# Three-stage seams of a fused attention and routed-leaf kernel: weights, rows and gathers issued in the stage before, output groups and an inverse moved between VectorE and POOL

## The chip, the cores and the metric

The kernel runs on one core of one Trainium2 chip. The metric is the device time of one execution in microseconds. Before the change the median of three runs is 4000.38 us (3998.59 to 4003.65). Engines: TensorE (PE, with its weight loads as PEld), VectorE (DVE), ScalarE (ACT), GpSimd (POOL), SyncE (SP), which only issues transfers here.

## The reference, cut to what matters

The input x is [8, 1024, 256] in float32. The output is x plus a differential attention and a fast-feedforward attention of the normalised x.

```python
xn = _layernorm(x)
# differential attention, 16 heads of 16, two maps per head
A1 = einsum('bhqd,bhkd->bhqk', Q1, K1) * scaling
A2 = einsum('bhqd,bhkd->bhqk', Q2, K2) * scaling
attn = softmax(A1) - lamb * softmax(A2)
out = einsum('bhqk,bhkd->bhqd', attn, V)          # then @ Wo, layernorm, gamma, beta
# feedforward: three trees (q, k, v), each token takes one of 16 leaves
cur = 2 * cur + 1 + (score >= 0)                  # four levels
hidden = relu(xf @ w1[leaf] + b1[leaf])           # 256 -> 64
y = hidden @ w2[leaf] + b2[leaf]                  # 64 -> 256
# then softmax(q k^T / 16) v per batch, over 1024 tokens
return x + attention(xn) + ffn_attention(xn)
```

## The kernel before

The program is four blocks that run one after the other, each with a barrier at its end: `route_stage` (layer norm, projections, routing of every token), `attention_stage`, `leaf_stage` and `mix_stage` (the softmax over the leaf outputs). Each block takes its own SBUF memory, and gives it back at its end; what passes between them goes through scratch tensors in HBM.

**Attention** handles 64 sets, eight of each of the eight batches; a set is two heads with two maps each, so four parts. A set has 16 steps (two halves of 512 queries, eight key tiles each). In a step TensorE writes four score tiles, ScalarE takes their exponentials (L1488), and TensorE multiplies by the values (L1358). For a later set TensorE writes row scores in advance (L1304) into one of three auxiliary banks, four a step, and VectorE reduces each to a row maximum (L1631) before the bank is free again. The same three banks carry the "extras", in an order written out by hand (`extras`, `GROUP_PLACES`, L1141): at step 5 and step 11 the finished values of a half are turned (`"o"`, `turn_o`), at step 12 the shift for the next set, and in sets 0 and 1 of a batch the turning and projection of the two output groups of the batch before. ScalarE reads a turned half with `read_o` (L1454). VectorE then inverts the row sums at step 7 or 13 (`invert`, L1641), and POOL multiplies by sign and inverse and adds the two maps (`join_maps`, L1528 to L1536); the result goes to `oset`, which the output groups are made of.

An output group is 512 tokens. VectorE takes its statistics in set 1 of the next batch, at step 1 (group 0) and step 14 (group 1), with `stats` (L1758 to L1763). POOL does the rest in `finish`: five small operations for the inverse deviation, beginning with a power (L1770 to L1778), and five over 4 x 256 columns (L1780 to L1793). SP stores the group. After the last batch both groups are done in the same way in an epilogue, and the block ends when the stores have landed. In the first half of a batch POOL also scatters the normalised rows to their sorted places (`scatter`, L1539).

**Leaf** runs over 240 tiles of 128 sorted tokens, 80 for each tree. A tile's leaf has a record of 641 words in SBUF; POOL copies the record of each tile out of all 16 (`choose`, L819) into a ring of eight (`WBUF`), and may be eight tiles ahead of VectorE. TensorE turns a pair of tiles (L757), multiplies by the first weights (L768) and the second (L779) in this order: turn of pair p, hidden of p - 1, output of p - 2. VectorE adds the bias (L835) into one of four store buffers (`YBUF`) of four tiles. SP issues loads of rows six groups of four tiles ahead (`XAHEAD`), the stores, and the weights of a tree, 5.25 MB, of which two sets fit:

```python
load(0)
nc.sync.dma_start(leafw[:, 0], w["leafw"][0]).then_inc(leafw_in[0], 16)
for g in range(1, XAHEAD):
    load(g)
nc.sync.dma_start(leafw[:, 1], w["leafw"][1]).then_inc(leafw_in[1], 16)
```

**Mix** takes one batch after the other. POOL gathers the rows of q, k and v with one indirect transfer for each 128 tokens (L919), eight of them for one input of a batch. TensorE turns q and k (`turn_rows`, L942), ScalarE and VectorE split them in two parts (L1002, L133), and scores, exponentials, turned probabilities and values follow.

Of the kernel before, what the change touches and what calls it, by code (L numbers as in the profile page):

```python
# [75 lines left out]
ROUTE_WORDS, LEAF_WORDS, MIX_WORDS, ATTENTION_WORDS = 38900, 40000, 21200, 40000  # L76
# [606 lines left out]
def leaf_stage(nc, ctx, ps, w, scratch):  # L683
# [3 lines left out]
    leafw = ar.take(2, LEAVES, REC)  # L687
    ident = ar.take(P)
    tablei = ar.take(TILES_ALL).bitcast(I32)
    xg = ar.take(XBUF, GROUP_T, DIM)  # L690
# [8 lines left out]
    leafw_in = [sem(f"leafw{f}_in") for f in range(NFFF)]  # L699
    ident_in, table_in = sem("ident_in"), sem("table_in")  # L700
    xg_in, y_stored = [sem(f"xg{n}_in") for n in range(XBUF)], [sem(f"y{n}_stored") for n in range(YBUF)]
# [13 lines left out]
    with nc.Block() as block:  # L715

        @block.sync
        def _(sp):
            nc.sync.dma_start(tablei[0:1], scratch["table"]).then_inc(table_in, 16)
            nc.sync.dma_start(ident, w["ident"]).then_inc(ident_in, 16)  # L720

            def load(g):
                if g >= XBUF:

                    sp.wait_ge(xT_full, (g - XBUF + 1) * GROUP_T // 2)
                tokens = scratch["sorted_x"][GROUP_T * P * g:GROUP_T * P * (g + 1)]
                nc.sync.dma_start(xg[:, g % XBUF], tokens.rearrange("(t p) d -> p t d", p=P)).then_inc(xg_in[g % XBUF], 16)

            load(0)
            nc.sync.dma_start(leafw[:, 0], w["leafw"][0]).then_inc(leafw_in[0], 16)  # L730
            for g in range(1, XAHEAD):
                load(g)
            nc.sync.dma_start(leafw[:, 1], w["leafw"][1]).then_inc(leafw_in[1], 16)
            for g in range(GROUPS):
                if g + XAHEAD < GROUPS:
                    load(g + XAHEAD)
                if (g + 1) * GROUP_T == TILES_F:

                    sp.wait_ge(wsel_ready, TILES_F)
                    nc.sync.dma_start(leafw[:, 0], w["leafw"][2]).then_inc(leafw_in[2], 16)  # L740
# [7 lines left out]
        def _(pe):  # L748
            def turn_pair(p):
# [5 lines left out]
                for n in range(2):  # L755
                    for k in range(KC):
                        last = nc.tensor.transpose(bank(p % 2)[:, (KC * n + k) * P:(KC * n + k + 1) * P],  # L757
                                                   xg[:, g % XBUF, 2 * p % GROUP_T + n, k * P:(k + 1) * P], ident)
# [24 lines left out]
            pe.wait_ge(ident_in, 16)  # L783
# [29 lines left out]
        def _(pool):  # L813
            def choose(n):
# [4 lines left out]
                nc.gpsimd.tensor_copy(wsel[:, n % WBUF], leafw[:, n // TILES_F % 2, bass.ds(leaf, 1)].rearrange("p a n -> p (a n)")  # L819
                                      ).then_inc(wsel_ready, 1)  # L820

            pool.wait_ge(table_in, 16)
# [16 lines left out]
def mix_stage(nc, ctx, ps, w, scratch, out):  # L839
# [4 lines left out]
    rows = ar.take(2, 2, TT, DIM)  # L844
# [4 lines left out]
    ident = ar.take(P)  # L849
    posi = ar.take(TOK_TILES, NFFF).bitcast(I32)  # L850
# [1073 lines left out]
```

## Time and profile before

| | us |
|---|---|
| median of three runs | 4000.38 |
| the profiled execution | 4000.26 |
| its span | 3998.4 |
| PE busy | 3750.3 (94%) |
| DVE busy | 3155.2 (79%) |
| ACT busy | 2784.6 (70%) |
| POOL busy | 1111.7 (28%) |

The page cuts the span in 40 slices of 100 us. Route is the first four, attention ends early in slice 32, the leaf stage ends in slice 34 and mix takes the rest. A share of busy time over the whole is an average over these stages; an engine's digit in a slice says what it does in that stage. Times in the rows are microseconds from the start of the span; "[... <-X]" behind a row is the idle time of the engine before it and what ended it.

### The profile page before, as it was taken

What the parts mean: (1) busy time and instruction counts of PE and PEld (TensorE: products, weight loads), DVE (VectorE), ACT (ScalarE), POOL (GpSimd) and SP (SyncE); (2) the same over time, 40 slices, a digit from 0 to 9 for tenths busy, and PEclk for the clock granted to TensorE, in tenths of its full rate; (3) what the DMA queues carried; (4) which work ended last, traced back from release to release, by engine and by line L of the source; (5) the groups of instructions that cost most, each with busy time, mean ns of one, the idle gap of its engine ahead of it and who ended that gap; (6) DMA issues with size and microseconds to landing.
All of it is one profiled execution on the core that took longest, in us unless ns stands there. A gap on an engine that the chain in (4) does not pass through costs nothing. (4 is left out here: it accounts for less than half of the span.)

```text
span 3998.4 us, 63421 instructions
## 1 busy us (share of the span) xinstructions
PE 3750.3 (94%) x23714; PEld 1469.9 (37%) x23714; DVE 3155.2 (79%) x5549; ACT 2784.6 (70%) x3257; POOL 1111.7 (28%) x1552
## 2 busy tenths in 40 slices
PE   7998999999999999999999999999999859799999
PEld 5772222222222222222222222222222235488888
DVE  6548899999989999998999999899999323345444
ACT  4440788888888888887888888788878836522221
POOL 3321141132113113211311321131131267662330
PEclk9996999999999999999999999999999979899999
DMA  8883110111111011111101111110100079732220
GB/s 289 308 294 98 40 44 28 48 42 38 39 45 43 28 47 42 38 42 42 43 28 53 37 38 44 40 43 28 51 29 29 22 285 324 237 116 72 88 85 22
DMA packets 224694, 330.89 MB, mean 83 GB/s; under 512 B 29297, under 2 KB 165236, under 8 KB 219780
## 3 DMA queue, kind: packets, MB, share of 16 engines
q1 hardware_dynamic: 205668, 276.08, 21.4%
q0 software_dynamic: 18432, 50.36, 3.9%
q8 instruction: 190, 3.11, 0.3%
q14 instruction: 116, 0.95, 0.1%
q10 hardware_dynamic: 288, 0.39, 0.1%
HBM read 169.34 MB, written 156.34 MB: 81 GB/s over the span
## 5 line engine op out<-in xcount | busy, mean ns | idle before, releaser
L1631 DVE TENSOR_REDUCE arena<-psum 128x1 f32<-128x512 f32 x4096 | 2559.4, 682 | 171.9 <-PE psum L1304 155.2
L1488 ACT ACTIVATE arena<-psum,exp_scale 128x1024 f32<-128x1024 f32 x2048 | 2157.6, 1110 | 297.6 <-PE psum L1342 287.2
L1304 PE MATMUL psum<-arena 48*128 48x512 f16 x4096 | 1313.8, 394 | 112.9 <-DVE arena L1631 35.2
L1358 PE MATMUL psum<-arena 128*32 128x512 f32 x8200 | 1106.2, 612 | 1.2 <-ACT arena L1488 0.6
L1304 PEld LDWEIGHTS psum<-arena 48*128 48x128 f16 x4096 | 317.1, 93 | 1764.1 <-DVE arena L1631 1492.4
L1342 PE MATMUL psum<-arena 50*128 50x512 f16 x4096 | 901.5, 384 | 15.4 <-ACT arena L1488 8.4
L1528 POOL TENSOR_TENSOR arena<-arena 128x16 f32<-128x16 f32 x129 | 28.4, 220 | 2078.4 <-DVE arena L1641 2078.4
L1016 ACT ACTIVATE mix_arena<-psum,mix_arena 128x1024 f32<-128x1024 f32 x64 | 71.3, 1114 | 328.9 <-DVE mix_arena L1036 328.9
L1358 PEld LDWEIGHTS psum<-arena 128*32 128x32 f32 x8200 | 162.1, 108 | 257.3 <-issue 255.7
L1342 PEld LDWEIGHTS psum<-arena 50*128 50x128 f16 x4096 | 213.7, 95 | 93.2 <-ACT arena L1488 78.8
L919 POOL DMA_INDIRECT mix_arena<-scratch_sorted_y,mix_arena x192 | 181.7, 946 | 235.1 <-PE psum L971 168.7
L835 DVE TENSOR_TENSOR leaf_arena<-psum,leaf_arena 128x256 f32<-128x256 f32 x240 | 90.5, 420 | 183.5 <-PE psum L779 170.5
L971 PE MATMUL psum<-mix_arena 128*128 128x256 f32 x1024 | 232.5, 380 | 2.7 <-DVE qk_lo L133 2.7
L1539 POOL DMA_INDIRECT scratch_sorted_x<-arena x192 | 188.5, 982 | 54.9 <-issue 54.9
L971 PEld LDWEIGHTS psum<-mix_arena 128*128 128x128 f32 x1024 | 189.6, 190 | 28.8 <-DVE qk_lo L133 5.6
L819 POOL COPY leaf_arena<-leaf_arena 128x641 f32 x240 | 168.4, 722 | 81.2 <-issue 41.9
L1035 DVE TENSOR_REDUCE mix_arena<-psum 128x1 f32<-128x1024 f32 x64 | 78.4, 1225 | 129.7 <-PE psum L141 129.7
L460 ACT ACTIVATE route_arena<-psum,route_arena 128x512 f16<-128x512 f32 x128 | 88.4, 691 | 117.7 <-PE psum L141 117.7
L555 DVE SCALAR_TENSOR_TENSOR route_arena<-psum,route_arena 128x512 f16<-128x512 f32 x128 | 95.7, 749 | 56.4 <-ACT route_arena L460 55.6
L806 ACT ACTIVATE leaf_arena<-psum 128x512 f32<-128x512 f32 x120 | 71.7, 597 | 95.0 <-PE psum L757 95.0
L1051 DVE SCALAR_TENSOR_TENSOR mix_arena<-psum,mix_arena 128x256 f32<-128x256 f32 x64 | 31.0, 484 | 117.2 <-PE psum L971 117.2
L757 PE MATMUL psum<-leaf_arena 128*128 128x128 f32 x480 | 80.6, 292 | 35.9 <-DMA leaf_arena<-scratch_sorted_x 35.9
(167 smaller groups left out, 3311.9 us busy)
## 6 DMA issues: line engine op xcount, KB each, us to landing
arena<-scratch_split SPq DMA_DIRECT2D x762, 64.0 KB
scratch_split<-route_arena SPq DMA_DIRECT2D x64, 512.0 KB, 3.3
scratch_sorted_x<-route_arena SPq DMA_DIRECT2D x60, 512.0 KB, 4.5
leaf_arena<-scratch_sorted_x SPq DMA_DIRECT2D x60, 512.0 KB, 6.0
scratch_sorted_y<-leaf_arena SPq DMA_DIRECT2D x60, 512.0 KB, 4.0
leaf_arena<-in_leafw SPq DMA_DIRECT2D x3, 5128.0 KB, 18.8
arena<-in_x SPq DMA_DIRECT2D x18, 512.0 KB, 4.9
scratch_sum<-arena SPq DMA_DIRECT2D x18, 512.0 KB, 2.9
```

The source lines that it names most:

```text
L460: nc.scalar.activation(parts[:, p % SPLIT_RING, 0, cols], unit_bank("qk", b, u), ACT.Identity, scale=lift[:, t, a:a + 1]).then_inc(act_rea ...
L555: nc.vector.scalar_tensor_tensor(parts[:, n, 1, cols], unit_bank("qk", b, u), lift[:, t, a:a + 1], parts[:, n, 0, cols], ALU.mult, ALU.sub ...
L819: nc.gpsimd.tensor_copy(wsel[:, n % WBUF], leafw[:, n // TILES_F % 2, bass.ds(leaf, 1)].rearrange("p a n -> p (a n)")).then_inc(wsel_ready, 1)
L835: nc.vector.tensor_tensor(yg[:, g % YBUF, n % GROUP_T], bank(4 + 2 * (n // 2 % 2) + n % 2)[:, 0:DIM], wsel[:, n % WBUF, B2], ALU.add).then ...
L919: nc.gpsimd.indirect_dma_start(dst, None, scratch["sorted_y"], bass.IndirectOffsetOnAxis(ap=posi[:, at, f:f + 1], axis=0)).then_inc(gather ...
L971: last = nc.tensor.matmul(bank[:, 0:DIM], probT[:, t % 2, kt, :], v[:, b % 2, kt, :], start=kt == 0, stop=kt == TT - 1)
L1304: nc.tensor.matmul(aux_bank[bank], ring[at, slot, 0, m, qt * P:(qt + 1) * P], ring[at, slot, 1, m, c * CH:(c + 1) * CH], start=True, stop=True
L1342: last = nc.tensor.matmul(score[:, 2 * m + h, :], ring[at, s % RING, 1, m, kt * P:(kt + 1) * P], ring[at, s % RING, 0, m, c * CH:(c + 1) * ...
L1358: last = nc.tensor.matmul(value_bank[32 * j:32 * j + 32, :], vaug[:, batch % 2, kt, 2 * pair + j % 2, :], prob[:, step % 2, j, :], start=k ...
L1488: nc.scalar.activation(prob[:, step % 2, 2 * h:2 * h + 2, :], score[:, 2 * h:2 * h + 2, :], ACT.Exp, scale=exp_scale[:, s % 2, s // 2:s // ...
L1539: nc.gpsimd.indirect_dma_start(scratch["sorted_x"], bass.IndirectOffsetOnAxis(ap=token_places[:, t, f:f + 1], axis=0), token_rows[:, t], N ...
L1631: nc.vector.tensor_reduce(halfmax[:, odd, 2 * m + h, qt, c:c + 1], aux_bank[bank], AX.X, ALU.max).then_inc(bank_used[bank], 1)
```

## The change

The inverse of the row sums is computed on POOL at the head of `join_maps`, as a power of -1 and one Newton step, so four operations more on POOL, and VectorE's `invert` with its waits is gone. POOL waits for ScalarE's read of the turned half itself. The finish of an output group is cut in two: `inverse_std` (the five small operations) and `finish` (the five large ones), and after the last batch VectorE runs `finish` for both groups, behind their statistics.

Two sets of buffers outlive a stage. `LeafStart` holds the first tree's weights, the identity, the table of leaves and two groups of rows; SP issues the first three in set 2 of the last batch and the rows after the last set, once all scatters have landed. `MixStart` holds the places and the q and k rows of two batches; the places are loaded in the leaf stage behind the second weights, and the 16 gathers of batch 0's q and k are issued by POOL in the leaf stage, one after each record copy from tile 184 on.

```diff
+class LeafStart:
+    SLOTS = 2
+    def load_weights(self, eng, w, scratch):
+        eng.dma_start(self.tablei[0:1], scratch["table"]).then_inc(self.table_in, 16)
+        eng.dma_start(self.ident, w["ident"]).then_inc(self.ident_in, 16)
+        eng.dma_start(self.leafw, w["leafw"][0]).then_inc(self.leafw_in, 16)
+    def load_rows(self, eng, scratch, g):
+        tokens = scratch["sorted_x"][GROUP_T * P * g:GROUP_T * P * (g + 1)]
+        eng.dma_start(self.xg[:, g], tokens.rearrange("(t p) d -> p t d", p=P)).then_inc(self.xg_in[g], 16)
+class MixStart:
+    def gather(self, eng, scratch, dst, b, f, t):
+        at = TT * b + t
+        eng.indirect_dma_start(dst, None, scratch["sorted_y"][0:(f + 1) * TILES_F * P],
+                               bass.IndirectOffsetOnAxis(ap=self.posi[:, at, f:f + 1], axis=0)
+                               ).then_inc(self.gathered[f][b % 2], 16)
...
 leaf_stage, SP
-            load(0)
-            nc.sync.dma_start(leafw[:, 0], w["leafw"][0]).then_inc(leafw_in[0], 16)
-            for g in range(1, XAHEAD):
+            for g in range(start.SLOTS, XAHEAD):
                 load(g)
-            nc.sync.dma_start(leafw[:, 1], w["leafw"][1]).then_inc(leafw_in[1], 16)
+            nc.sync.dma_start(leafw[1], w["leafw"][1]).then_inc(leafw_in[1], 16)
+            mix.load_places(nc.sync, scratch)
...
 leaf_stage, POOL
+            first = 2 * TILES_F + 24
             for n in range(TILES_ALL):
                 if n % TILES_F == 0:
                     pool.wait_ge(leafw_in[n // TILES_F], 16)
                 choose(n)
+                if n == first:
+                    pool.wait_ge(mix.posi_in, 16)
+                    for m in range(YBUF):
+                        pool.wait_ge(y_stored[m], 16 * (2 * TILES_F // GROUP_T // YBUF))
+                if first <= n < first + 2 * TT:
+                    f, t = divmod(n - first, TT)
+                    mix.gather(nc.gpsimd, scratch, mix.rows[:, 0, f, t], 0, f, t)
...
 mix_stage, POOL
+                    if b == 0 and f < 2:
+                        continue
...
 attention_stage, SP
+                    if s == 2 and tail:
+                        leaf.load_weights(nc.sync, w, scratch)
...
             for i in range(BATCH):
                 body(i, i == LAST)
+            sp.wait_ge(scattered, BATCH * (16 * TT * NFFF))
+            for g in range(leaf.SLOTS):
+                leaf.load_rows(nc.sync, scratch, g)
...
 attention_stage, POOL
             def join_maps(n, s, c):
-                pool.wait_ge(inverse_ready, n + 1)
+                total, done = osum[:, c, :, :, HD], n * 6
+                nc.gpsimd.tensor_tensor(linv[:, c], total, minus_one, ALU.pow).then_inc(ochain, 1)
+                nc.gpsimd.tensor_tensor(lres, linv[:, c], total, ALU.mult).then_inc(ochain, 1)
+                nc.gpsimd.tensor_scalar(lres, lres, -1.0, 2.0, ALU.mult, ALU.add).then_inc(ochain, 1)
+                nc.gpsimd.tensor_tensor(linv[:, c], linv[:, c], lres, ALU.mult).then_inc(ochain, 1)
...
+                    wait_read(pool, place(i, s, 5, "o", 1))
                     join_maps(2 * n, (s - 1) % PER_BATCH, 1)
...
+                    wait_read(pool, place(i, s, 11, "o", 0))
                     join_maps(2 * n + 1, s, 0)
...
+            wait_read(pool, START[BATCH] + EPILOGUE.index(("o", 1)))
             join_maps(BATCH * 2 * PER_BATCH, PER_BATCH - 1, 1)
             for h in range(2):
-                groups[h].finish(nc, pool, BATCH)
+                groups[h].inverse_std(nc, pool, BATCH)
...
 attention_stage, VectorE
-                        if step == 7:
-                            wait_read(dve, place(i, s, 5, "o", 1))
-                            invert(1)
-                        if step == 13:
-                            wait_read(dve, place(i, s, 11, "o", 0))
-                            invert(0)
...
+            for h in range(2):
+                groups[h].finish(nc, dve, nc.vector, BATCH)
```

Each operation on the chain waits for the one before it by a semaphore, as it did.

## Rows read from the trace of the kernel before

**Rows 1.** Page, busy tenths in 40 slices of 100 us, engine and DMA.

```profile
DVE  6548899999989999998999999899999323345444
...
DMA  8883110111111011111101111110100079732220
```

**Rows 2.** Groups by line, VectorE, 1500 to 3100 us: count, busy us, mean ns, idle.

```profile
L1631 DVE TENSOR_REDUCE arena<-psum 128x1 f32<-128x512 f32 x2349 | 1468.7, 682 | 91.8 <-PE psum L1304 82.1
L1641 DVE RECIPROCAL arena<-arena 128x16 f32<-128x16 f32 x73 | 17.8, 244 | 0.0
```

**Rows 3.** Timeline, VectorE, one set of attention: start us, length us, instruction, count.

```profile
2616.10 0.24 DVE L1641 RECIPROCAL arena<-arena 128x16 f32<-128x16 f32 x1
2616.26 9.28 DVE L1631 TENSOR_REDUCE arena<-psum 128x1 f32<-128x512 f32 x15
```

**Rows 4.** Timeline, all engines, set 1 of a batch, around group 1's statistics.

```profile
2578.68 0.40 ACT L1454 ACTIVATE arena<-psum 128x272 f32<-128x272 f32 x1
...
2586.38 0.22 POOL L1528 TENSOR_TENSOR arena<-arena 128x16 f32<-128x16 f32 x1 [16.48 <-DVE arena L1641]
...
2587.79 1.05 POOL L1770 TENSOR_TENSOR arena<-arena 128x4 f32<-128x4 f32 x1
...
2590.04 1.89 POOL L1780 TENSOR_TENSOR arena<-arena 128x1024 f32<-128x1024 f32 x1
2590.39 1.56 DVE L1763 TENSOR_SCALAR arena<-arena 128x4 f32<-128x4 f32 x1
...
2592.61 0.39 PE L1304 MATMUL psum<-arena 48*128 48x512 f16 x1 [2.81 <-DVE arena L1631]
```

**Rows 5.** Timeline, VectorE, the same batch, end of group 0's statistics.

```profile
2550.30 0.17 DVE L1763 TENSOR_SCALAR arena<-arena 128x4 f32<-128x4 f32 x1
```

**Rows 6.** Groups by line and form, whole span: powers on POOL, a tensor-tensor on VectorE.

```profile
L1770 POOL TENSOR_TENSOR arena<-arena 128x4 f32<-128x4 f32 x18 | 18.7, 1040 | 3.8 <-DVE arena L1763 3.8
...
L492 POOL TENSOR_TENSOR route_arena<-route_arena 128x8 f32<-128x8 f32 x8 | 13.3, 1658 | 161.2 <-DVE route_arena L537 161.2
...
L676 DVE TENSOR_TENSOR route_arena<-route_arena 1x1280 f32<-1x1280 f32 x3 | 4.4, 1477 | 0.1
```

**Rows 7.** Timeline, all engines, end of attention and first issue of the leaf stage.

```profile
3185.88 0.25 DVE L1641 RECIPROCAL arena<-arena 128x16 f32<-128x16 f32 x1 [11.00 <-ACT arena L1454]
...
3188.75 1.04 PE L1740 MATMUL psum<-arena 128*128 128x128 f32 x8
...
3196.12 1.47 DVE L1763 TENSOR_SCALAR arena<-arena 128x4 f32<-128x4 f32 x1
...
3215.77 2.34 POOL L1793 TENSOR_TENSOR arena<-arena 128x1024 f32<-128x1024 f32 x1
...
3224.89 0.25 SPq L719 DMA_DIRECT2D leaf_arena<-scratch_table  x1
```

**Rows 8.** Timeline, all engines, start of the leaf stage.

```profile
3242.81 5.41 POOL L819 COPY leaf_arena<-leaf_arena 128x641 f32 x8 [24.70 <-issue]
...
3248.79 0.76 DVE L835 TENSOR_TENSOR leaf_arena<-psum,leaf_arena 128x256 f32<-128x256 f32 x2 [51.19 <-PE psum L779]
...
3251.10 0.66 PE L768 MATMUL psum<-leaf_arena 128*64 128x128 f32 x8
...
3265.85 1.42 DVE L835 TENSOR_TENSOR leaf_arena<-psum,leaf_arena 128x256 f32<-128x256 f32 x4 [3.62 <-DMA scratch_sorted_y<-leaf_arena]
```

**Rows 9.** Timeline, POOL, steady leaf stage.

```profile
3305.94 2.77 POOL L819 COPY leaf_arena<-leaf_arena 128x641 f32 x4 [0.80 <-DVE leaf_arena L835]
```

**Rows 10.** Timeline, all engines, start of mix.

```profile
3475.11 0.36 SPq L889 DMA_DIRECT2D mix_arena<-scratch_posi  x1
...
3479.14 0.95 POOL L919 DMA_INDIRECT mix_arena<-scratch_sorted_y,mix_arena  x1 [0.30 <-issue]
...
3489.51 3.65 PE L942 MATMUL psum<-mix_arena 128*128 128x128 f32 x16 [18.64 <-DMA mix_arena<-scratch_sorted_y,mix_arena]
...
3504.50 0.80 PE L139 MATMUL psum<-qk_hi 128*128 128x512 f32 x1 [1.41 <-DVE qk_lo L133]
```

More of the change, by code:

```diff
@@ new lines, with __init__, load_places @@
+class MixStart:
+    def __init__(self, nc, ctx):
+        ar = Arena(ctx.enter_context(nc.sbuf_tensor("mix_start", [P, MIX_START_WORDS], F32)))
+        self.rows = ar.take(2, 2, TT, DIM)
+        self.posi = ar.take(TOK_TILES, NFFF).bitcast(I32)
+        self.posi_in = ctx.enter_context(nc.semaphore("m_posi_in"))
+        self.gathered = [[ctx.enter_context(nc.semaphore(f"m_gathered{f}_{n}")) for n in range(2)] for f in range(NFFF)]
+    def load_places(self, eng, scratch):
+        eng.dma_start(self.posi.rearrange("p (b t) f -> p b t f", b=BATCH), scratch["posi"].rearrange("b p t f -> p b t f")
+                      ).then_inc(self.posi_in, 16)
+    def gather(self, eng, scratch, dst, b, f, t):
[3 more added lines that the diff above has]
+                               ).then_inc(self.gathered[f][b % 2], 16)
@@ L686, in leaf_stage @@
+def leaf_stage(nc, ctx, ps, w, scratch, start, mix):
     ar = Arena(ctx.enter_context(nc.sbuf_tensor("leaf_arena", [P, LEAF_WORDS], F32)))
[L687 to L690, printed above, removed]
+    leafw = (start.leafw, ar.take(LEAVES, REC))
+    ident, tablei = start.ident, start.tablei
+    later = ar.take(XBUF - start.SLOTS, GROUP_T, DIM)
+    xg = [start.xg[:, n] for n in range(start.SLOTS)] + [later[:, n] for n in range(XBUF - start.SLOTS)]
@@ L836, in _, with mix_stage @@
                                         wsel[:, n % WBUF, B2], ALU.add).then_inc(y_ready, 1)
-def mix_stage(nc, ctx, ps, w, scratch, out):
+def mix_stage(nc, ctx, ps, w, scratch, out, leaf, start):
     qk = Split(nc, ctx, "qk", [2, KC, SEQ])
     ar = Arena(ctx.enter_context(nc.sbuf_tensor("mix_arena", [P, MIX_WORDS], F32)))
-    rows = ar.take(2, 2, TT, DIM)
+    rows, posi, ident = start.rows, start.posi, leaf.ident
     v = ar.take(2, TT, DIM)
@@ L854, in sem @@
         return ctx.enter_context(nc.semaphore("m_" + name))
-    ident_in, posi_in = sem("ident_in"), sem("posi_in")
-    gathered = [[sem(f"gathered{f}_{n}") for n in range(2)] for f in range(NFFF)]
+    gathered = start.gathered
     sum_in, out_stored = [sem(f"sum{n}_in") for n in range(2)], [sem(f"out{n}_stored") for n in range(2)]
@@ L1068, in _, with attention_stage @@
                         value(one, n)
-def attention_stage(nc, ctx, base, ps, w, scratch, out, exp_scale):
+def attention_stage(nc, ctx, base, ps, w, scratch, out, exp_scale, leaf):
     ar = Arena(base)
@@ L1081, in attention_stage @@
     linv = ar.take(NCH, 4, PARTS)
+    lres, minus_one = ar.take(4, PARTS), ar.take(4, PARTS)
     omul = ar.take(4, PARTS, HD)
```

112 lines of the change are left out of this document (55 added, 57 removed).

## The prediction

> **What bounds the kernel now.** I read the page first, for the stages: VectorE is at nine tenths through attention, and the DMA engines are at nine tenths only in the leaf stage [rows 1]. Then I read the groups by line inside attention: VectorE spends 1468.7 of 1600 us in the maxima of L1631 and 17.8 us in reciprocals [rows 2]. Its timeline shows fifteen maxima in 9.28 us, 0.62 us each, with no wait among them, and the reciprocal sitting in that stream [rows 3]. So in most steps of attention VectorE sets the pace and TensorE waits for a bank. Around the two places where a group's statistics are taken the timeline of all engines shows TensorE waiting 2.81 us for VectorE [rows 4]. Last I read the two gaps between stages, where nobody computes: from the end of attention to the first bias add of the leaf stage [rows 7, 8], and from the leaf stage to the first scores of mix [rows 10]. The sums below are against the profiled execution, 4000.26 us with a span of 3998.4 us; the median of the three plain runs is 4000.38 us, so the two can be used as one.
>
> **Reciprocals leave VectorE.** The reciprocal starts 0.16 us before the next maximum [rows 3], so 0.15 us of the stream goes with each. Removing it pays only where VectorE paces. In sets 2 to 7 of a batch the stream has no turn or projection in it, which gives 6 sets x 2 x 0.15 = 1.8 us a batch. In sets 0 and 1 VectorE waits for TensorE anyway and I count nothing. The last three sets have no maxima, so 7.6 batches count: 7.6 x 1.8 = 13.7 us. Bounds: 0 if TensorE has no slack to follow, and 73 reciprocals x 0.16 us x 128/73, about 20 us, if all pay. I take 13.7, since the stream of rows 3 has no idle in it. The work isn't free on POOL: one power of 4 columns takes 1.040 us and one of 8 takes 1.658 [rows 6], which is 0.154 us a column, so 16 columns should take 2.9 us (an estimate). With three short operations of 0.2 us and gaps of 0.08 that is 3.7 us in front of each join, which itself lasts 1.41 us (from 2586.38 to 2587.79, [rows 4]). Two joins of 5.1 us in a set leave POOL under half busy, and it now starts at ScalarE's read (step 5 or 11) and not at steps 7 and 13. The added wait on POOL for that read has the split of the maxima, the group finish and the scatters queued behind it; by these times they start no later than before. Hidden, at 0 us; if POOL were late the shift would hold all of TensorE.
>
> **The same move shifts POOL under VectorE's statistics.** In set 1 of every batch VectorE ends a group's statistics with the small L1763. It took 0.17 us with POOL idle [rows 5] and 1.56 us with POOL inside L1780, ending within 0.02 us of L1780's own end (2590.04 + 1.89) [rows 4]. So it waits for whatever elementwise operation POOL is in, and TensorE's gap of 2.81 us holds that wait. After the change POOL starts at 2579.1 (ScalarE's read, 2578.68 + 0.40), and is through the inverse and the join at 2579.15 + 3.7 + 1.6 = 2584.4. L1780 then starts 2.25 us later (the distance 2587.79 to 2590.04), L1783 1.97 us after that, and ends at 2590.5. L1763 arrives at about 2590.25, a reciprocal earlier than now, and waits some 0.3 to 0.5 us in place of 1.4. That is 1 us a batch, 8 us in eight. But L1786 starts right behind L1783 and lasts 2.35 us: if POOL is only 0.25 us quicker than I reckon, L1763 meets that one, waits 2.3 us, and this term turns to +8. Bounds -12 (no wait, all eight) and +8. I take -8.
>
> **End of attention.** The last join's reciprocal is on the path now. Before, ScalarE's read ended at 3185.88 and TensorE turned group 1 at 3188.75, not waiting for POOL [rows 7]. After, the join ends 5.3 us past the read, at 3191.2, so group 1 comes 2.5 us later. Its statistics ended at 3196.3 less the POOL wait (L1763 0.17 in place of 1.47), so at 3198.8 now. Then both groups' finish run on VectorE behind them, ten operations over 1024 columns. VectorE's tensor-tensor of 1280 columns took 1.477 us [rows 6], so 1.18 us each and 1.22 with the wait on the chain: 12.2 us, which ends at 3211.0. POOL's end was 3218.11 (3215.77 + 2.34), and the first issue of the leaf stage came 6.8 us after it, at 3224.89 [rows 7]; that distance is the last store, its landing and the barrier, and it stays. Gain 7.1 us, bounds 4 and 10. The first group is ready when the second's statistics are done, so its finish is delayed for nothing; it isn't the last.
> By the Trainium skill (GPSIMD Engine Reference, Key points) GpSimd shares its SBUF interfaces with VectorE and contends with instructions that have two SBUF inputs, which all ten finish operations have. Rows 4 and 5 show such a wait for L1763, which has one input; no row shows a two-input one meeting POOL here. If VectorE had to wait out POOL's inverse of group 1, this term would be 2.25 us poorer, which lies inside its bounds.
>
> **Start of the leaf stage.** Now POOL can copy its first record only at 3242.81, when the 5.25 MB of weights have landed, and the first bias add is at 3248.79, 23.9 us after the stage's first issue [rows 7, 8]. After the change weights, identity, table and the first eight tiles are in SBUF. What stays is two turned pairs at low clock and the chain of 6.0 us from the first copy to the first bias add (3242.81 to 3248.79), 6.6 us with the turn that has to come first. Gain 17.3 us; bounds 13 (the engines need time to enter the block that the DMA wait hides now) and 18. The weights are loaded in the last batch, behind set 2's shift, where DMA is at one tenth [rows 1]; behind them on SP are a group store and the next split parts, which are needed two sets (80 us) later. 0 us.
>
> **The second weights come sooner, relatively.** VectorE waits 3.62 us at 3265.85 for the first output store, which is queued behind the second 5.25 MB [rows 8]. From the stage's first issue 41.0 us passed for 14.7 MB (two weights, seven row groups, one store). After it is 8.5 MB: at the same rate with 4 us of fixed latency 25 us. Now the ninth pair is due at 3248.79 + 8 x 1.81 = 3263.3 and comes 2.6 us late. After, it is due 6.6 + 8 x 1.81 = 21.1 us in and comes 3.9 us late. I charge the difference, rounded to 1.4 us, bounds 0 and 6.
>
> **Gathers inside the leaf stage.** Sixteen gathers are put between POOL's record copies at tiles 184 to 199, and POOL isn't idle there: four copies take 2.77 us and wait 0.80 us for VectorE in the 3.62 us that TensorE needs for two pairs [rows 9], so it has 0.2 us a tile to spare. A gather costs 0.95 us and 0.30 us behind it [rows 10], 1.25 us. POOL's lead is the ring of eight records: the copy for a pair ends 5.7 us before that pair's bias add (four pairs, 7.2 us, less 0.76 and 0.8), and TensorE wants it 3.1 us before (the hidden layer of the fourth pair at 3251.10, its bias add at 3248.79 + 3 x 1.81 = 3254.2) [rows 8]. Lead 2.5 us. 16 x 1.25 = 20.0, less 17 tiles x 0.2 = 3.5, less 2.5 gives 14 us of TensorE waiting, not recovered later because TensorE paces the stage. Bounds 8 (the 0.30 us hides behind the copies and a store's slack is used) and 18 (1.5 us a gather under full DMA). The waits for the places and for the stores of the first 40 groups come 24 tiles, 22 us, late: 0.
>
> **Start of mix.** Scores begin at 3504.50, 29.4 us after the stage's first issue at 3475.11; TensorE's first turn waits for eight gathers until 3489.51 [rows 10]. With rows, places and identity present the turns start with the stage; four of the eight units take 3.65 us and the first score 1.41 us more [rows 10], so it comes 7.3 + 1.4 = 8.7 us into the stage. Gain 20.7 us, bounds 18 and 22. Values of batch 0 need eight gathers, 12.8 us into the stage, and are read 22 us into it: hidden.
>
> **Sum.** -13.7 - 8 - 7.1 - 17.3 + 1.4 + 14 - 20.7 = -51.4 us, from 4000.3: 3949 us.
>
> **Rivals.** (1) The statistics meet POOL's 2.35 us operation: +8 in place of -8, 3965 us. For it: the margin is a quarter of a microsecond and rests on an extrapolated power. Against: both nearest rows lie on one line. Chance 0.20. (2) TensorE doesn't follow VectorE in attention, since its own step is nearly as long: 13.7 us less, 3963 us. Against it stand the stretches without idle of rows 3. Chance 0.12. (3) Gathers fit better than reckoned, 8 us in place of 14: 3943 us. Chance 0.09. (4) Slower: issue of a gather is held by the DMA queues, which run at nine tenths in the leaf stage [rows 1], and POOL with it. The change is lost from 51.4 / 16 = 3.2 us more a gather, 4.5 us each; at 6 us it is +76 - 51, 4025 us. Against: a gather into idle queues shows no such hold. Chance 0.03. (5) The leaf stage doesn't start on what is preloaded, as entering the block or the next rows take the time: half of the 17 us, 3958 us. Chance 0.06. The forecast has 0.50.
>
> **Numbers.** The forecast and rivals 1, 2, 3 and 5 are all faster. What a measurement of this kernel can tell from no change is about 0.2%, 8 us. The range 3933 to 3970 takes in rivals 1 to 3 and 5 with the bounds of the gathers. Faster 0.95, within 0.2% 0.02, slower 0.03.
>
> **What would show it.** Right: no reciprocals on VectorE; values of L1763 in set 1 well under 1.5 us; a power of some 2.9 us on POOL; the leaf stage's first bias add 6 to 7 us after its first issue; a stretch of 16 gathers in which record copies come every 1.9 us and TensorE is about half busy; scores 9 us into mix. Wrong: L1763 at 2 us or more; a power far from 2.9 us; copies and gathers in one 0.9 us tile; a later wait for stores over 10 us.

## The result, and the profile after

The changed kernel takes 3961.04 us (median of 4 runs, 3959.20 to 3962.41) against 3999.89 us beside it (4 runs): ratio 0.9902, 95% interval 0.9889 to 0.9914, so 38.9 us faster. The prediction was 3949, with 3933 to 3970. The spans of the profiled executions are 3957.3 and 3998.4 us, 41.1 apart.

The page of after has the same shape as [rows 1]: VectorE at nine tenths in attention, the DMA engines only in the leaf stage, here slices 32 to 34.

```profile
DVE  6548899999989999998999899899989533344444
...
DMA  8883110111011011101101110110102169742220
```

By line, the reciprocals of [rows 2] are gone from VectorE and POOL has the power in their place; first the 1600 us that answer to [rows 2] (VectorE, 1490 to 3090 us), then two lines of the whole span: POOL's power of 16 columns, and VectorE's small add, the one-input operation at the end of a group's statistics (L1763 before).

```profile
L1690 DVE TENSOR_REDUCE arena<-psum 128x1 f32<-128x512 f32 x2352 | 1475.1, 684 | 100.5 <-PE psum L1350 91.4
```
```profile
L1574 POOL TENSOR_TENSOR arena<-arena 128x16 f32<-128x16 f32 x129 | 376.9, 2921 | 1518.8 <-ACT arena L1500 1518.8
...
L1812 DVE TENSOR_SCALAR arena<-arena 128x4 f32<-128x4 f32 x18 | 3.1, 174 | 0.6
```

The 17.8 us of reciprocals in that window came back as idle time (91.8 to 100.5) and as maxima that take 684 ns and not 682, more than as shorter attention. The power is 2.921 us (estimate 2.9), the small add never waits (0.174 us, mean of before 0.862).

Timeline of after around group 1's statistics, to be read against [rows 4] (start, length; in brackets the idle time before and who ended it):

```profile
2569.49 2.91 POOL L1574 TENSOR_TENSOR arena<-arena 128x16 f32<-128x16 f32 x1 [10.81 <-ACT arena L1500]
...
2578.99 1.89 POOL L1835 TENSOR_TENSOR arena<-arena 128x1024 f32<-128x1024 f32 x1
2580.31 0.38 DVE L1810 BATCH_NORM_AGGREGATE arena<-arena 128x2 f32<-128x6 f32 x4
2580.72 0.18 DVE L1812 TENSOR_SCALAR arena<-arena 128x4 f32<-128x4 f32 x1
...
2580.96 2.35 POOL L1837 TENSOR_TENSOR arena<-arena 128x1024 f32<-128x1024 f32 x1
2581.55 0.39 PE L1350 MATMUL psum<-arena 48*128 48x512 f16 x1 [1.43 <-DVE arena L1690]
...
2583.28 1.94 PE L1404 MATMUL psum<-arena 128*32 128x512 f32 x8
...
2586.72 1.06 PE L1404 MATMUL psum<-arena 128*32 128x512 f32 x8
```

The add ends at 2580.90, with POOL's L1835 (2580.88) and 0.06 us before L1837, the operation of 2.35 us, starts. TensorE's gap is 1.43 us and not 2.81. What follows had no term in my sum: eight value matmuls take 1.94 us behind the gap and 1.06 a step later, which is TensorE at the lower of its two clocks (1.2 GHz) and at full clock again. A step of the attention loop whose value matmuls take 1.9 us is called a slow step below. At group 0, 40 us earlier, the gap is the 1.42 us it always was, but two steps are slow:

```profile
2540.11 0.39 PE L1350 MATMUL psum<-arena 48*128 48x512 f16 x1 [1.42 <-DVE arena L1690]
...
2541.84 1.93 PE L1404 MATMUL psum<-arena 128*32 128x512 f32 x8
...
2545.64 1.94 PE L1404 MATMUL psum<-arena 128*32 128x512 f32 x8
2549.13 1.06 PE L1404 MATMUL psum<-arena 128*32 128x512 f32 x8
```

The granted clock of this stretch, and of the next. The columns are busy us and count of PE, PEld, DVE, ACT and POOL, then clock, DMA share and GB/s:

```profile
2541.20:2547.60 6.40, 6.40 (x28) 1.14 (x29) 4.33 (x8) 3.86 (x4) 0.00 (x0) 0.50 0.00 0
2549.20:2557.00 7.80, 7.62 (x56) 1.96 (x57) 7.51 (x13) 6.60 (x8) 4.84 (x7) 1.00 0.01 2
```

To compare kernels I take the starts of ScalarE's 129 reads of attention outputs (L1454 before, L1500 after). Eight of the intervals hold group 0's statistics, eight hold group 1's; the rest is called plain. In us:

| kernel | plain | with group 0 | with group 1 |
|---|---|---|---|
| before | 2277.5 | 239.2 | 251.5 |
| after | 2272.4 | 247.3 | 237.1 |
| difference | -5.1 | +8.0 | -14.4 |

End of attention and start of the leaf stage, to [rows 7, 8]:

```profile
3173.19 0.41 ACT L1500 ACTIVATE arena<-psum 128x272 f32<-128x272 f32 x1
...
3179.16 1.85 PE L1789 MATMUL psum<-arena 128*128 128x128 f32 x8 [2.51 <-POOL arena L1590]
...
3185.94 1.41 DVE L1807 BATCH_NORM_STATS2 arena<-arena 128x6 f32<-128x256 f32 x4 [6.81 <-ACT arena L1803]
...
3187.87 1.22 DVE L1833 TENSOR_TENSOR arena<-arena 128x1024 f32<-128x1024 f32 x1
3188.04 1.91 POOL L1818 TENSOR_TENSOR arena<-arena 128x4 f32<-128x4 f32 x1 [6.69 <-DVE arena L1812]
...
3193.01 1.18 POOL L1826 TENSOR_TENSOR arena<-arena 128x4 f32<-128x4 f32 x1
...
3199.26 1.23 DVE L1842 TENSOR_TENSOR arena<-arena 128x1024 f32<-128x1024 f32 x1
3203.91 2.02 SPq L771 DMA_DIRECT2D leaf_arena<-scratch_sorted_x  x4
...
3206.63 0.47 SPq L720 DMA_DIRECT2D mix_start<-scratch_posi  x1
3207.15 9.54 SPq L771 DMA_DIRECT2D leaf_arena<-scratch_sorted_x  x1
3210.53 0.76 DVE L887 TENSOR_TENSOR leaf_arena<-psum,leaf_arena 128x256 f32<-128x256 f32 x2 [10.05 <-PE psum L822]
...
3216.72 6.10 SPq L786 DMA_DIRECT2D scratch_sorted_y<-leaf_arena  x1
...
3228.97 1.42 DVE L887 TENSOR_TENSOR leaf_arena<-psum,leaf_arena 128x256 f32<-128x256 f32 x4 [5.03 <-DMA scratch_sorted_y<-leaf_arena]
```

From ScalarE's last read to the first issue of the leaf stage 30.7 us pass (39.4 before), from there to the first bias add 6.6 (23.9). The leaf stage itself, first to last bias add, takes 243.0 us for 222.1. How late the stage is at a store group (four tiles) I read from the issue of its output store, against the first bias add and 1.81 us a pair. After the second weights (group 19) it was 1.3 us late before and is 6.8 now; at group 30, after the third weights, 8.5 and 13.0; at group 50, past the gathers, 8.5 and 29.3. In the stretch of gathers POOL takes a copy and a gather every 1.87 us without a pause, and TensorE is busy for 21.0 of 32 us (3390 to 3422):

```profile
3407.30 0.72 POOL L862 COPY leaf_arena<-leaf_start 128x641 f32 x1
3407.59 0.76 DVE L887 TENSOR_TENSOR leaf_arena<-psum,leaf_arena 128x256 f32<-128x256 f32 x2 [2.98 <-PE psum L822]
3408.19 0.97 POOL L725 DMA_INDIRECT mix_start<-scratch_sorted_y,mix_start  x1 [0.17 <-DVE leaf_arena L887]
```

Mix, to [rows 10]: the first score comes 12.0 us after the last bias add (33.6 before).

```profile
3457.73 6.04 PE L984 MATMUL psum<-leaf_start,mix_start 128*128 128x128 f32 x32 [4.26 <-PEq L762]
...
3465.51 0.50 PE L140 MATMUL psum<-qk_hi 128*128 128x512 f32 x1 [1.74 <-DVE qk_lo L134]
```

The stretches add up to the 41.1: prologue of attention -0.8, its body -11.4, its end -8.7, leaf start -17.3, leaf stage +20.9, mix start -21.6, the rest of mix -2.1. The last can't be put down to the change: with the mix code of before, the rest of mix takes from 492.2 to 494.1 us in four kernels (493.9 in the kernel before), and 491.8 here.

### The profile page after: what moved, and what is told of

Same layout as the page of the kernel before. It is cut to its first block and busy times, and to the rows that moved or that the text cites. A ratio compares the mean times of both kernels' runs of the same rounds, so it can differ in the third digit from the quotient of the medians.

```text
span 3957.3 us, 63809 instructions
## 1 busy us (share of the span) xinstructions
PE 3748.4 (95%) x23714; PEld 1471.3 (37%) x23714; DVE 3146.5 (80%) x5431; ACT 2784.3 (70%) x3257; POOL 1558.3 (39%) x2058
## 5 line engine op out<-in xcount | busy, mean ns | idle before, releaser
L1574 POOL TENSOR_TENSOR arena<-arena 128x16 f32<-128x16 f32 x129 | 376.9, 2921 | 1518.8 <-ACT arena L1500 1518.8
L725 POOL DMA_INDIRECT mix_arena<-scratch_sorted_y,mix_start x64 | 60.5, 946 | 192.7 <-PE psum L1013 167.3
L725 POOL DMA_INDIRECT mix_start<-scratch_sorted_y,mix_start x128 | 121.5, 949 | 36.8 <-issue 34.3
L862 POOL COPY leaf_arena<-leaf_start 128x641 f32 x160 | 111.8, 723 | 47.4 <-issue 25.0
```

What stands on the lines that cost most here:

```text
L725: eng.indirect_dma_start(dst, None, scratch["sorted_y"][0:(f + 1) * TILES_F * P], bass.IndirectOffsetOnAxis(ap=self.posi[:, at, f:f + 1], ...
L862: nc.gpsimd.tensor_copy(wsel[:, n % WBUF], leafw[n // TILES_F % 2][:, bass.ds(leaf, 1)].rearrange("p a n -> p (a n)")).then_inc(wsel_ready, 1)
L1574: nc.gpsimd.tensor_tensor(linv[:, c], total, minus_one, ALU.pow).then_inc(ochain, 1)
```

## The experiments

Each was timed in five rounds beside the kernel before (3999.4 to 4000.0 us). Its table of intervals is read as the one above. Kernels with the same attention differ in their number of slow steps (see the part on the clock), so two medians can be some microseconds apart by this alone; where a stretch is given, it is from the profiled execution.

**Why only 5 of 13.7 us from the reciprocals.** `e1_inverse_only` is the kernel before with the inverse moved to POOL and nothing else (L1574 to L1580 of after in join_maps, invert removed).

> The kernel before with one part of the change: the inverse of the row sums made on POOL. Theory A (the trace of after read as it stands): attention to its last read gains 11 to 12 us (5 in the plain sets, 14 at group 1's statistics, minus 8 at group 0's, where TensorE's clock stays low for longer), and the end of attention loses about 1 us (the last join 2.5 us later, the wait of the small add 1.3 shorter): 3989 to 3990 us. My prediction's terms: 13.7 + 8 - 1, 3979. If part of the 11 us came from the other edits of the change (memory layout, the loads of the leaf weights), it is 3994 or more.

Measured 3989.18 us, ratio 0.9967 (0.9956 to 0.9978), the first theory's time, but not by its parts. Plain 2272.4, group 0 239.9, group 1 248.8. The plain part is after's, with a gain of 5.1 us. The groups are not: the add waits no more (0.2 us) and TensorE's gap is 1.46 us and not 2.81, but all eight of group 1's intervals have two slow steps now, so that 2.7 us are left where the theory had 14. Attention to the last read gained 7.1 us in the profiled execution (3992.04), not 11 to 12. Three of the seven runs lie at 3983 to 3985 and four at 3989 to 3992, so that the median meets the theory is partly chance.

`e2_no_inverse` leaves out the division, so that POOL's share is short as well:

```
...
-                pool.wait_ge(inverse_ready, n + 1)
-                nc.gpsimd.tensor_tensor(linv[:, c], linv[:, c], sign, ALU.mult)
+                nc.gpsimd.tensor_tensor(linv[:, c], osum[:, c, :, :, HD], sign, ALU.mult)
```

> The kernel before without any inverse of the row sums: POOL multiplies with the sums themselves (this leaves out the division). VectorE loses its reciprocals and POOL gets no longer. Why did the plain sets give 5 us in place of 13.7? Theory A, TensorE doesn't follow VectorE: the maxima of L1631 keep 682 ns, the plain intervals between two reads of ScalarE gain 5 us again, and VectorE's idle time grows; group 1's small add meets POOL's fourth finish operation and waits 1.4 us as before, so nothing comes from there: 3993 us. Theory B, POOL's longer work slows VectorE's maxima (684 ns against 682 over 3750 maxima is 7.5 us): here they keep 682 and the plain intervals gain 13: 3985 us.

Measured 3989.32 us, 0.9974 (0.9963 to 0.9984); plain 2272.5. In the same 1600 us as [rows 2] VectorE shows

```profile
L1633 DVE TENSOR_REDUCE arena<-psum 128x1 f32<-128x512 f32 x2355 | 1476.5, 684 | 94.7 <-PE psum L1304 82.9 <-issue 2.4
```

684 ns with no power on POOL at all, so POOL doesn't slow the maxima. TensorE doesn't follow: that was my rival 2. I had said that the maxima keep 682, which is wrong; the mean rises when the reciprocals leave, with POOL busy or not. The whole came 4 us under my 3993. In the profiled execution, beyond the 5.0 us of the plain sets, 2.4 us are in the intervals of the groups (241.5 and 246.8; the add waited 1.0 us there and not 1.4), 1.2 in the leaf stage and 1.5 in mix, whose code e2 doesn't touch.

**The gap at the statistics.** `e5_stats_split` takes the lump apart, with finer places for each piece:

```
+STATS_PLACES = (((0, 9), (0, 10), (0, 11), (0, 12)), ((1, 10), (1, 11), (1, 12), (1, 14)))
+JOIN_PLACES = ((0, 14), (1, 15))
-                            if (s, step) == (1, 1 if h == 0 else 14):
-                                groups[h].stats(nc, link)
...
+                            if (s, step) in STATS_PLACES[h]:
...
+                                link(groups[h].moments(nc, q))    # one bn_stats
+                            if (s, step) == JOIN_PLACES[h]:
+                                groups[h].join_moments(nc, link)
```

> The kernel after with each group's statistics on VectorE taken apart: its four bn_stats one each in the steps that follow the reads of the projected tiles, the joining and the small add one step later, in place of one lump of 1.95 us. Theory A: TensorE's gap of 1.42 us in each group exists only because the lump is longer than the lead of the three banks, and its clock falls after such a gap, for no, one or two steps at 1.3 us more each, which is what moved group 0's and group 1's intervals by +8 and -14. Then both go: 22.7 us of gaps and some 20 to 30 us of slow steps, 3910 to 3920 us. Theory B: the clock falls there for another reason (the turns and projections); only the gaps go, 3938 us. Theory C: VectorE has no slack in those steps, the same time is lost in smaller waits: 3957 us or more.

Measured 3923.65 us, 0.9811 (0.9798 to 0.9825): 37 us under after. Plain 2272.3, group 0 220.7, group 1 227.8 (two pieces of group 0 and one of group 1 stand in intervals that count as plain, which did not grow). In all eight batches group 0 has no gap left, and no slow value step is left in either group. Theory A holds in its mechanism, but its 3910 to 3920 us were too low: of the 36 us, 17.6 are gaps (8 x 1.42 and 8 x 0.78) and 18 slow steps, where I had 22.7 and 20 to 30. In group 1 a gap of 0.64 us stays. The timeline shows whose it is:

```profile
2551.03 2.36 POOL L1848 TENSOR_TENSOR arena<-arena 128x1024 f32<-128x1024 f32 x1
...
2552.58 0.83 DVE L1823 TENSOR_SCALAR arena<-arena 128x4 f32<-128x4 f32 x1
```

The small add, moved, has met POOL's 2.36 us operation again, and ends with it (2553.41 and 2553.39): my rival 1, on another kernel.

`e9_before_stats_split` is the same edit on the kernel before.

> The kernel before with nothing but the statistics taken apart. Does this gain need the change? The reciprocals stay on VectorE (5 us in the plain sets). Theory A: the gaps and the slow steps go here too: the 16 intervals with statistics fall from 490.7 to about 450 us, 3959 us, as much as the whole change. Theory B: group 1's small add at step 15 still meets POOL's finish of group 0 and waits 1.4 to 2.3 us, a gap remains, and with it the fall of the clock: 12 to 20 us of it stay, 3971 to 3979 us.

Measured 3951.64 us, 0.9879 (0.9864 to 0.9894): more than the whole change, and better than either theory. Plain 2277.2, as before; group 0 220.7, group 1 222.5. The add took 0.17 us at the end of a POOL operation and no gap stays. As its join stands at the same step as e5's, the 0.64 us that stay in e5 come from the add's wait and not from the place or the number of VectorE's operations. The two columns give back 47.5 us: 33.8 of gaps (8 x 2.81 and 8 x 1.42, against 40 us that I had for all) and the rest slow steps.

**The gathers.** `e3_gathers_late` removes them from the leaf stage's POOL loop and lets mix make all of batch 0's.

> The kernel after with its sixteen gathers back at the start of mix; places, identity and rows stay resident. The leaf stage gives back 16.3 us (the lateness from tile 184 on), and the start of mix loses 8 gathers of 1.25 us, their landing of 2 us and the turn at low clock: 12 to 15 us. So this part of the change by itself is worth next to nothing or less: 3957 us, range 3955 to 3961. By my prediction's terms, 14 us for the gathers, and 20.7 us for the start, it is 3968.

Measured 3964.52 us, 0.9911 (0.9898 to 0.9925). The leaf stage has its 16.2 us back (226.8), and mix's first score comes 31.7 us after the last bias add: 19.7 lost where I expected 12 to 15 (and 3964.5 us for 3955 to 3961), since TensorE waits for both sets of eight, 16 x 1.25 us.

```profile
3450.72 3.68 PE L974 MATMUL psum<-leaf_start,mix_start 128*128 128x128 f32 x16 [16.62 <-DMA mix_start<-scratch_sorted_y,mix_start]
...
3460.72 3.68 PE L974 MATMUL psum<-leaf_start,mix_start 128*128 128x128 f32 x16 [6.32 <-DMA mix_start<-scratch_sorted_y,mix_start]
```

So moving the gathers, as it was done, is worth 3.5 us by the two stretches. `e4_gathers_spread` issues them so:

```
-            first = 2 * TILES_F + 24
...
-                if first <= n < first + 2 * TT:
...
+            firsts, every = (TILES_F + 24, 2 * TILES_F + 24), (9, 7)
+                for f in range(2):
...
+                    t, rest = divmod(n - firsts[f], every[f])
+                    if rest == 0 and 0 <= t < TT:
+                        mix.gather(nc.gpsimd, scratch, mix.rows[:, 0, f, t], 0, f, t)
```

> The kernel after with the sixteen gathers spread: eight at every ninth record from tile 104, eight at every seventh from tile 184. Theory A, the cost is POOL's time (0.97 us and 0.17 behind it, against 0.2 us a tile to spare and a ring of 8 records): 7 to 9 tiles give 1.4 to 1.8 us for the 1.14 of a gather, nearly all hides, the 16.3 us fall to 0 to 3: 3945 to 3948 us. Theory B, the cost is in the DMA queues, which are full until the last row loads: the first eight cost as much there, and it is 3953 to 3961.

Measured 3945.91 us, 0.9863 (0.9848 to 0.9878), as theory A had it. From group 30 on the stage loses 3.5 us in place of 16.3, and TensorE's pace (1.05 us of idle ahead of each pair of bias adds) is kept around a gather:

```profile
3390.75 0.97 POOL L725 DMA_INDIRECT mix_start<-scratch_sorted_y,mix_start  x1
3391.43 0.76 DVE L889 TENSOR_TENSOR leaf_arena<-psum,leaf_arena 128x256 f32<-128x256 f32 x2 [1.05 <-PE psum L822]
```

**The weights.** `e6_weights_in_parts`:

```
-            nc.sync.dma_start(leafw[1], w["leafw"][1])
...
+            for f, at in ((1, 1), (2, TILES_F // GROUP_T - 1)):    # in the loop over groups
+                if 0 <= g - at < 16 and (g - at) % 2 == 0:
...
+                    load_chunk(f, (g - at) // 2)                   # two of 16 leaves
```

> The kernel after with the second and third 5.25 MB of leaf weights loaded in eight parts each, two row groups apart, in place of one transfer each. The leaf stage is 6.8 us late after the second weights and 14.8 after the third. Theory A, order: the stall is that of stores and row loads queued behind one long transfer, and parts let them through: 8 to 11 us come back, 3950 to 3953 us. Theory B, capacity: rows in and out fill the queues to 0.96 at TensorE's pace as it is, so 10.5 MB more at some 330 GB/s cost their time in whatever order: 0 to 3 us, 3958 to 3961 us.

Measured 3946.60 us, 0.9868 (0.9853 to 0.9884): order, not capacity. The stage is 1.7 us late at group 19 (after: 6.8) and 2.6 at group 30 (after: 13.0). Stores and row loads pass between the parts:

```profile
3220.88 1.19 SPq L779 DMA_DIRECT2D leaf_arena<-in_leafw  x1
3220.96 0.76 DVE L892 TENSOR_TENSOR leaf_arena<-psum,leaf_arena 128x256 f32<-128x256 f32 x2 [1.05 <-PE psum L827]
...
3223.55 0.36 SPq L791 DMA_DIRECT2D scratch_sorted_y<-leaf_arena  x1
```

For the second weights it doesn't separate two causes, because it also put the load of the places ahead of them.

`e8_no_leaf_start` undoes the preloads.

> The kernel after with the leaf stage's first weights, rows, identity and table loaded in the leaf stage again, as before. The first bias add comes 23.9 us after the stage's first issue and not 6.6: 17.3 us more. By my prediction 1.4 of it come back at the second weights, 3977 us. By the trace of after, where the stage is 6.8 us late after the second weights and the kernel before was 1.4 late, 5 come back: 3973 us.

Measured 3977.90 us, 0.9944 (0.9930 to 0.9957). First issue to first bias add 23.6 us, so the 17 us are the preloads'. But nothing came back: 7.3 us late at group 19, with the weights, rows and stores in the order of the kernel before, which was 1.3. The earlier start isn't the cause. What this kernel has beyond before is the load of the places; `e10_places_later` moves it to group 32.

> The kernel after with one line moved: the 96 KB load of the gathers' places is issued at row group 32 of the leaf stage and not right behind the second weights. Open is what makes the stage 6.8 us late there and not 2.7 as predicted; the kernel without the leaf preloads is 7.3 us late too, the kernel before 1.3, so it isn't the earlier start. Theory A, the places: the load has over a thousand packets of under 512 bytes, the row load issued next was held for 9.54 us and the store after it for 6.10. Then the stage is 1.5 to 3.5 us late at group 19, and the whole 3956 to 3958 us. Theory B, the long weight transfer alone: 6.8 us late as now, 3961 us. The same few microseconds turning up at group 32 would say that the load costs them wherever it stands.

Measured 3953.09 us, 0.9880 (0.9863 to 0.9896), 8 us under after. How much of the 8 is the places' the medians don't say: in the profiled execution (3957.64) the leaf stage is 5.1 us shorter than after's and the intervals of the groups are 4.5 us longer. The stage is 2.6 us late at group 19, as theory A had it. SP's queue behind the second weights, as against the 9.54 and 6.10 us above:

```profile
3209.75 0.54 SPq L775 DMA_DIRECT2D leaf_arena<-in_leafw  x1
3210.34 0.45 SPq L771 DMA_DIRECT2D leaf_arena<-scratch_sorted_x  x1
3217.10 0.36 SPq L787 DMA_DIRECT2D scratch_sorted_y<-leaf_arena  x1
3217.50 9.21 SPq L771 DMA_DIRECT2D leaf_arena<-scratch_sorted_x  x1
```

One issue of 9 us stands behind the second weights here too, as in the kernel before (8.11 us); but it comes behind the first store, which goes out at once, and the second one, of 6.10 us, is gone. In after the long issue comes one transfer earlier, and the first store is behind it. At group 32 the places cost no more than 0.4 us.

**The end of attention.** `e7_finish_order`:

```
+            nc.vector.reciprocal(linv[:, 1], osum[:, 1, :, :, HD]).then_inc(last_inverse, 1)
             for h in range(2):
...
                 groups[h].stats(nc, link)
+                if h == 0:
+                    groups[0].finish(nc, dve, nc.vector, BATCH, range(0, 3))
-            for h in range(2):
-                groups[h].finish(nc, dve, nc.vector, BATCH)
+            groups[0].finish(nc, dve, nc.vector, BATCH, range(3, 5))
+            groups[1].finish(nc, dve, nc.vector, BATCH)
```

> The kernel after with two things changed at the very end of attention: the last reciprocal is back on VectorE, and three of the first group's five finish operations run on VectorE before the second group's statistics, where it was idle for 6.81 us; the other two fill POOL's inverse for the second group. Expected by the timeline: 2.5 us (TensorE's turn of group 1 no longer waits for POOL's join) and 3 operations of 1.26 us less what the finish pushes the statistics: 5 to 6.5 us in all, 3955 us. If VectorE's operations with two inputs and POOL's small ones hinder each other more than now (POOL's inverse took 6.3 us in place of 2.3), 2 to 3 us: 3958.

Measured 3955.34 us, 0.9888 (0.9873 to 0.9903). From the last read to the leaf stage's first issue 26.9 us for 30.7: 3.8, between the two. Of these 1.2 us are TensorE's clock: in e5 and e10, with after's own epilogue, the same turn comes behind the same gap of 2.51 us at full clock (1.07 us in e10 for 1.85), and from the read to the issue both take 29.5 us. By them the new order is worth 2.6 us. I had left out that the first group's finish waits for POOL's inverse:

```profile
3186.18 3.74 DVE L1851 TENSOR_TENSOR arena<-arena 128x1024 f32<-128x1024 f32 x3 [2.27 <-POOL arena L1837]
...
3191.93 1.91 POOL L1829 TENSOR_TENSOR arena<-arena 128x4 f32<-128x4 f32 x1 [5.79 <-DVE arena L1823]
...
3195.18 6.26 DVE L1851 TENSOR_TENSOR arena<-arena 128x1024 f32<-128x1024 f32 x5 [0.94 <-POOL arena L1837]
```

**All together.** `b1_all` has the split statistics, the spread gathers, the weights in parts and the new finish; `b2_all_join_later` also JOIN_PLACES = ((0, 14), (2, 2)).

> Four edits together on the kernel after: statistics taken apart, gathers spread, weights in parts, the finish reordered. If they add up, by the stretches measured one at a time: attention 36 us, the weights 9, the gathers 13, the end of attention 3.8, 62 us from 3961: 3898 to 3900 us. If the spread gathers and the weight parts compete for the same queues in the second third of the leaf stage, 5 to 8 us less: 3905 us.

> The same with the joining of group 1's statistics and its small add three steps later, at step 2 of set 2, past the bn_stats of step 14. One theory: the gap of 0.65 us that is left in group 1 comes from two additions to VectorE within two steps, and goes: 8 x 0.65 is 5 us, 3893 to 3895 us. The other: set 2 is as full on VectorE, the gap only moves: the same as its sibling within 1 us in the attention stretch.

Measured 3900.70 us, 0.9750 (0.9737 to 0.9763), and 3893.86 us, 0.9735 (0.9721 to 0.9748). The parts add up, and the last gap goes with the later join (group 1 222.5 us for 227.7, gap 0.64 to none; the add takes 0.17 us). The second is the best version: 106 us under before, 67 under after, mean granted clock 0.985 for 0.974. From 500 to 3100 us, the columns are length, PE, PEld, DVE, ACT and POOL busy (count), clock, DMA share and GB/s, first after, then this one:

```profile
500.00:3100.00 2600.00, 2509.81 (x16664) 623.53 (x16660) 2441.16 (x4026) 2218.03 (x2305) 1036.86 (x1416) 0.99 0.14 42
```
```profile
500.00:3100.00 2600.00, 2525.47 (x16883) 627.70 (x16882) 2453.92 (x4057) 2251.51 (x2341) 1049.91 (x1436) 1.00 0.13 42
```

## Why the prediction was right, and where it was not

The range held and the forecast was 12 us too low (3949 for 3961); rival 2's 3963 was nearer. Term by term, from the profiled executions:

| term | predicted | measured |
|---|---|---|
| reciprocals, plain sets | -13.7 | -5.1 |
| group 1's statistics | -8 | -14.4 |
| group 0's statistics | none | +8.0 |
| end of attention | -7.1 | -8.7 |
| start of the leaf stage | -17.3 | -17.3 |
| second weights | +1.4 | +5.5 |
| gathers | +14 | +16.3 |
| start of mix | -20.7 | -21.6 |
| prologue, third weights, rest of mix | none | -0.8, -0.9, -2.1 |

Some terms came out 23 us poorer than the sum had them (reciprocals 8.6, group 0 8.0, second weights 4.1, gathers 2.3), others 13 us better. That the total lies 10 us off and not 23 is luck.

- **Reciprocals.** The step that failed is "the stream of rows 3 has no idle in it", taken for a whole set. Between two reads 15.56 and 26.12 us passed in a plain set, 41.7 us; VectorE's 64 maxima at 0.62, one join and two reciprocals fill 40.2. TensorE's own step is 2.49 us (2586.72 to 2589.21 and on in the trace of after), as long as four maxima. So each set gained 0.10 us at one of its reciprocals and 0.01 at the other, where the sum had 0.15 at each. e1 and e2 show it: 5.1 and 5.0 us with POOL's inverse and with none. Rival 2 was the case for the greater part (5.1 of 13.7 us came), and its chance of 0.12 was too small.
- **Group 1.** The wait of the small add went as described, all of it (8 x 1.38 = 11 us), by a margin of 0.06 us, and with luck: the sum puts 3.7 us for the inverse and 1.6 for the join, whose own row gives 1.41; they took 3.89 and 1.41, so the two errors cancel in 5.3. That the add may meet the next POOL operation is shown by e5. The other 3 us are slow steps.
- **The clock.** No term of the sum had it, though [rows 4] has the gap that sets it off. Behind a gap of 1.4 us TensorE ran no, one or two slow steps, 1.1 to 1.4 us more for each. That the gap sets it off is shown by taking it away: in every kernel that has the 16 gaps of 1.4 us or more, all slow steps stand in their intervals, and with no gap over 0.65 us (e5, e9, b1, b2) there is none and the granted clock is 1.00 from 500 to 3100 us. How many steps are slow is not settled by the code: before has 14, after 19, e1, e7 and e10 24. After, e3, e4, e6 and e8 have 246 to 249 us with group 0 and 235 to 237 with group 1, e1, e7 and e10 with the same instructions in attention's body 239.9 to 240.0 and 248.8 to 248.9; the timed runs of e10 fall at 3948 to 3950 and 3956 to 3958. What decides between these is open.
- **End of attention and leaf start.** As worked out: TensorE's turn waited 2.51 us for POOL's join (2.5), ten operations of 1.22 us that start every 1.26 (1.22 in the sum), 6.6 us to the first bias add. The rest of the gain at the end, 1.6 us, is the shorter way from the last operation to the first issue, 3.4 us where it had been 6.8, against 0.4 us for the ten starts and statistics that ended 1.4 us later than I reckoned, TensorE's turn and projection being at its lower clock (the turn 1.85 us for 1.04). I had called the 6.8 us the last store, its landing and the barrier, and kept them. The step was wrong: before, that store had landed at 3221.03, but POOL's drain at the end of the block lasted until 3224.65, 6.54 us behind POOL's last operation. After, the drain takes the same 6.54 us but ends at 3200.72, and the store's landing at 3203.43 is last. So 3.4 us come from VectorE, and not POOL, doing the last operations, and no term had them.
- **Second weights.** The 1.4 us were right: e10 is 2.6 us late where before was 1.3. The load of the places, which I costed only for POOL's wait (at 0), costs 4.2 us where it stands on SP's queue. e8 and e10 show it.
- **Gathers.** 0.97 us and 0.17 behind it in place of 1.25. A copy and a gather take POOL 1.87 us where TensorE's pace is 0.905 a tile, 15.4 us for sixteen, so the 2.5 us of lead that I took off don't show in the 16.3; where they went no run says. TensorE was at its lower clock for a part of the stretch (granted clock 0.84 from 3390 to 3422 us). In e5, e7 and e10 the same sixteen cost 14.6 us, so 14 was near what this stretch does; that it would nearly cancel their gain was in my own two terms (14 and, by e3, 19.7 of the 20.7), and is the place where the change could have had 13 us more.

## What to carry to other kernels

A stream without idle on one engine isn't the pace of the loop: compare the period of the loop with the sum of that engine's work in a period before pricing what leaves it. A lump of 2 us on the pacing engine cost its gap and the clock after it; cutting it into pieces, each in a step of its own, was worth more here than the whole change (48 us for 39). When an engine's work at the end of a block moves to another, read what the block's end waits for: here it was POOL's drain and not the last store. Price every DMA that is moved, small ones too, by what stands behind it on its queue, and spread work over an engine's slack rather than putting it in one block.

## What the runs showed of the hardware

- POOL's elementwise power: 1.02 to 1.05 us for 4 columns with VectorE quiet, 1.66 for 8 [rows 6], 2.92 for 16.
- VectorE's operations with two SBUF inputs and POOL's small ones at the same time: VectorE kept 1.22 to 1.23 us, POOL's 0.20 us became 1.17 to 1.18, its power 1.91 for 1.02. POOL is the one that loses here. VectorE's small add with one input is the other way round: it waits for the end of POOL's operation (0.83 us in e5, 1.56 in [rows 4]). By the Trainium skill (SBUF — State Buffer, Who interferes with whom) the pair of ports that the two share is an exclusive lock, and the order of issue decides who waits; it names VectorE's tensor_scalar in a two-port mode beside the operations with two SBUF inputs. The trace agrees in both directions: POOL's small operations there ended some 0.05 us after the VectorE operation that had started before them, and the small add ends with POOL's. At the end of attention it hit POOL and not the path, so the 2.25 us that I allowed for it did not come.
- Behind a transfer of 5.25 MB one of SP's next issues takes 8 to 10 us (8.11 before, 9.54 after, 9.21 in e10). With a load of 96 KB in pieces of 96 bytes in between, it came one transfer earlier and a second of 6.10 us followed (e8 has the same pair, 9.78 and 6.13); at group 32 that load cost at most 0.4 us.
- POOL's drain at the end of attention lasts until 6.54 us after POOL's last operation in all fourteen kernels, and the block doesn't end before it.
